# A graph network kernel: one 128-node window per tile of edges, one-hots made by ScalarE, and duplicates and degrees moved from the relational loop into the attention loop

## What is computed

```python
deg = segment_sum(ones, dst); hw = einsum('nd,rdf->rnf', h, weight_r)
M = segment_sum(hw[etype, src] / deg[dst], dst)              # layer 0, relational
updated = relu(0.2 * h + 0.8 * M)
...
e = tanh(concat(h[src], h[dst]) @ W_attn.T + b_attn) @ w_out # layer 1, attention
alpha = softmax of e over the edges of one dst
z = segment_sum(alpha * h[src], dst)
...
deg = segment_sum(edge_weight, src); w = -dis[src] * edge_weight * dis[dst]
# layer 2: two Chebyshev propagations with w, gates, tanh; layer 3: one more propagation
```

## Time and profile before

| | us |
|---|---|
| median of the runs | 2011.47 |
| lowest, highest of 3 | 2008.94, 2014.19 |
| span of the profiled execution | 2533.2 |

### The profile page before, as it was taken

How to read it: one execution, slowest core, us unless ns; L and a number is a source line. 1 busy time by engine, 2 the same in 40 slices (tenths; PEclk the granted TensorE clock), 3 DMA queues, 4 the chain that set the end, 5 groups by cost and what they waited for, 6 DMA issues and landing times.

```text
span 2533.2 us, 28723 instructions
## 1 busy us (share of the span) xinstructions
PE 1374.4 (54%) x7844; PEld 1089.7 (43%) x7845; DVE 991.2 (39%) x2889; ACT 200.8 (8%) x390; POOL 1235.7 (49%) x1381
## 2 busy tenths in 40 slices
PE   4455555565621556566555651111111898879877
PEld 2455554554511456556555640000000898434423
DVE  7555554554604333334333440000000676300488
ACT  2000000000000111111111100000000111000200
POOL 1666666666672366565666677677777000000000
PEclk8766767677755555555555555555555898899989
DMA  5444343435200222222222200000000002988878
GB/s 165 150 155 153 120 152 118 150 121 168 65 1 0 68 63 66 65 62 64 66 66 64 66 21 0 0 0 1 0 0 0 0 0 103 353 335 353 326 295 336
DMA packets 154645, 272.07 MB, mean 107 GB/s; under 512 B 44030, under 2 KB 100154, under 8 KB 151546
## 3 DMA queue, kind: packets, MB, share of 16 engines
q1 hardware_dynamic: 111322, 229.57, 24.9%
q0 software_dynamic: 40064, 41.32, 6.6%
q10 hardware_dynamic: 3232, 0.82, 0.1%
HBM read 215.32 MB, written 56.29 MB: 107 GB/s over the span
## 4 chain that ended last, share of the span: by engine, by line
another core or an unknown queue 28%; PE 26%; issue 20%; DVE 14%; POOL 5%; DMA 4%; DVEq 1%; ACT 1%; SPq 1%; POOLq 0%; ACTq 0%
PE acc L987 10%; PE acc L1035 7%; POOL rings L736 5%; PE acc L1029 4%; DVE rings L1367 2%; DVE big L1826 2%; DMA big<-pairs_by_src 2%; DVE rings L1401 2%; DVE rings L1402 1%; DVE big L1391 1%; DMA rings<-local_rows 1%; PE acc L1009 1%; DMA relation_rows<-big 1%; DMA rings<-relation_rows,idx_ring 1%
## 5 line engine op out<-in xcount | busy, mean ns | idle before, releaser
L987 PE MATMUL acc<-rings 128*65 128x128 f32 x3328 | 576.1, 326 | 634.4 <-issue 459.6
L987 PEld LDWEIGHTS acc<-rings 128*65 128x65 f32 x3328 | 456.0, 168 | 709.4 <-issue 694.3
L736 POOL DMA_INDIRECT rings<-relation_rows,idx_ring x416 | 409.5, 984 | 281.9 <-issue 184.1
L736 POOL DMA_INDIRECT rings<-attention_rows,idx_ring x416 | 394.6, 948 | 305.1 <-issue 234.3
L1029 PE MATMUL acc<-attend_mem,rings 128*128 x1664 | 373.8, 411 | 266.2 <-issue 182.3
L1029 PEld LDWEIGHTS acc<-attend_mem,rings 128*128 128x128 f32 x1664 | 367.3, 328 | 273.0 <-issue 273.0
L753 POOL DMA_INDIRECT pairs_by_src<-fed_val,fed_idx x416 | 405.6, 975 | 149.4 <-issue 120.0
L1425 DVE TENSOR_SCALAR rings<-iota_bf,col_local,score 128x256 f32<-128x256 bf16 x416 | 139.4, 408 | 480.3 <-remote 371.8
L786 POOL DMA_INDIRECT big<-support_rows,ext_node x4 | 3.9, 963 | 450.6 <-DMA support_rows<-big 449.7
L1680 DVE TENSOR_TENSOR rings<-acc,rings 128x512 f32<-128x512 f32 x52 | 35.6, 684 | 352.0 <-remote 343.9
L1035 PE MATMUL acc<-big,attend_mem 128*64 128x512 f32 x700 | 163.0, 600 | 9.1 <-DMA big<-pairs_by_src 9.1
(11 more groups left out here) (279 smaller groups left out, 895.0 us busy)
## 6 DMA issues: line engine op xcount, KB each, us to landing
big<-pairs_by_src SPq DMA_DIRECT2D x54, 2048.0 KB, 12.5
pairs_by_src<-zeros SPq DMA_DIRECT2D x24, 1792.0 KB
big<-key_rows SPq DMA_DIRECT2D x52, 512.0 KB
rings<-local_rows SPq DMA_DIRECT2D x52, 256.0 KB
big<-pairs_by_src SPq DMA_DIRECT2D x12, 1024.0 KB, 12.3
rings<-relation_rows,idx_ring POOLq DMA_INDIRECT x416
pairs_by_src<-fed_val,fed_idx POOLq DMA_INDIRECT x416
rings<-attention_rows,idx_ring POOLq DMA_INDIRECT x416
```

The lines of the kernel that those rows point to most:

```text
L736: pool.indirect_dma_start(ring[h][:, u, 0:width], None, table, bass.IndirectOffsetOnAxis(ap=idx_ring[h][:, u:u + 1], axis=0),).then_inc(ga ...
L987: m = pe.matmul(node_sums[:, bass.ds(at[u] * P + w * P, P)], rows[h][:, u, :], onehot[h][:, u, w * P:(w + 1) * P], start=False, stop=False ...
```

## The change

- A tile's window starts at its own first destination, not at its block, and is 128 nodes wide. The sums lie in eight PSUM banks that overlap by 128 columns (384 new ones each), so that a window never crosses a bank; `turn_nodes` adds the overlaps (57 matmuls for 50). Relational and aggregation loop: one matmul of 128 columns per tile for two.
- In the relational loop ScalarE makes the one-hots, as relu(1 - |window place - column|): eight Abs instructions of 128 elements and one Relu of 1024 in a half-step. DVE has no work in the loop but the duplicates of the first 64 tiles (`early_dups`: three instructions of 1024 elements in each of 8 half-steps).
- Duplicates and degrees of all tiles move to the attention loop: DVE compares keys in one instruction of 1024 elements, makes the one-hot of the source's lower part in another, of its block in one of 200 and multiplies three of 200; PE adds 8 + 8 matmuls to each half-step; SP adds 512 KB of keys; ScalarE adds two small copies. Duplicates are all written to the same cell with the same sum; `indices` and the dump cells are gone.
- The look-up is one matmul of 128 columns per tile for two of 64. It fetches both blocks' numbers, and DVE picks by a predicated copy of 512 elements. One DVE instruction of 1024 elements makes the eight tiles' one-hots, for eight instructions of 256.
- In the aggregation loop DVE makes six of the eight weighted one-hots, ScalarE two (two Abs, two Relu).
- The zeroing writes 896 KB in each half-step for 1792 KB in each loop turn. The degrees' square roots move behind the aggregation loop.

```diff
@@ add_up
-                            block_at[0:1, bass.ds(it * (2 * H) + h * H, H)], ...
+                            sum_at[0:1, bass.ds(it * (2 * H) + h * H, H)], ...
...
-                            for w in range(2):
-                                m = pe.matmul(node_sums[:, bass.ds(at[u] * P + w * P, P)], rows[h][:, u, :],
-                                              onehot[h][:, u, w * P:(w + 1) * P], ...
+                            m = pe.matmul(node_sums[:, bass.ds(at[u], P)], rows[h][:, u, :], onehot[h][:, u, :], ...
-                        if key == "rel":
-                            pe.wait_ge(dups_read, it * 2 + h + 2)
-                            for u in range(H):
-                                m = pe.matmul(dup_bank[:, u * 7:(u + 1) * 7], eq[h][:, u, :], ...
@@ ScalarE, relational loop
+            def window_hots(it, h):
+                act.wait_ge(rows_free["rel"], it * 4 + 2 * h + 2)
+                for u in range(H):
+                    o = act.activation(onehot[h][:, u, :], iota_bf[:, 0:P], ACT.Abs, scale=-1.0,
+                                       bias=col_window[:, bass.ds(it * (2 * H) + (h * H + u), 1)])
+                o.then_inc(away_ready, 1)
+                act.wait_ge(away_ready, it * 2 + h + 1)
+                act.activation(onehot[h], onehot[h], ACT.Relu, scale=-1.0, bias=1.0).then_inc(onehot_ready["rel"], 1)
@@ look_up
                         for u in range(H):
+                            m = pe.matmul(found[h][:, u * 2 * D:(u + 1) * 2 * D], onehot_t[h][:, u * P:(u + 1) * P], there, ...
                         m.then_inc(slot_free[key], 1)
+                        pe.wait_ge(hots_ready, it * 2 + h + 2)
+                        for u in range(H):
+                            pe.matmul(degree_bank, onehot_lo[h][:, u, :], hi_parts[h][:, u, :], ...
+                        for u in range(H):
+                            m = pe.matmul(dup_bank[h][:, u, :], eq[h][:, u, :], parts_ring[h][:, u, :], ...
+                        m.then_inc(degrees_added, 1)
@@ score_step, behind the one-hots of the next half-step
+                    take_dups(it, h)
+                    tile_hots(it, h)
                     dve.wait_ge(gathered["att"][h], (it + 1) * (16 * H))
                     dve.wait_ge(slot_free["att"], it * 2 + h + 3)
+                    dve.copy_predicated(both[:, :, 0], upper_ring[h][:, :].unsqueeze(2).to_broadcast([P, H, D]), both[:, :, 1]
+                                        ).then_inc(picked, 1)
+                    dve.wait_ge(picked, it * 2 + h + 1)
+                    dve.tensor_tensor(msg[h][:, :, :], both[:, :, 0], rows2[h][:, :, 0:D], ALU.add).then_inc(bank_read, 1)
@@ tile_hots
+                dve.wait_ge(keys_here[h], (it + 1) * 16)
+                dve.tensor_tensor(eq[h], key_ring[h], key_cols[:, cols].unsqueeze(2).to_broadcast([P, H, P]),
+                                  ALU.is_equal).then_inc(keys_read, 1)
...
+                dve.tensor_tensor(onehot_lo[h], iota_bank.unsqueeze(1).to_broadcast([P, H, P]),
+                                  col_lo[:, cols].unsqueeze(2).to_broadcast([P, H, P]), ALU.is_equal)
@@ POOL
+            scatter(EARLY, T, dup_val[:, H:], dups_ready, EARLY // H + 5, 2 * IT + 1)
@@ weighted_hots
-                        for u in range(H):
+                        for u in range(BY_DVE):
```

More of the change, by code:

```diff
@@ L56, in gnn_kernel @@
     VB = N // P
+    SPAN = BANK - P
+    TOP = VB * P
+    SUM_BANKS = 8
+    assert SUM_BANKS * SPAN == TOP and SPAN % P == 0 and NODES == TOP + P
+    PER_SPAN = SPAN // P
     SLOTS = 6
@@ L367, in gnn_kernel @@
         sums_taken = {k: sem(f"sums_taken_{k}") for k in sum_passes}
-        dups_read = sem("dups_read")
+        early_read = sem("early_read")
+        early_here = [sem(f"early_here{h}") for h in range(2)]
+        early_eq_ready = sem("early_eq_ready")
+        early_ready = sem("early_ready")
+        away_ready = sem("away_ready")
+        neg_ready = sem("neg_ready")
+        weighted_away = sem("weighted_away")
+        hots_by_act = sem("hots_by_act")
+        key_cols_ready = sem("key_cols_ready")
+        parts_ready = sem("parts_ready")
+        dups_ready = sem("dups_ready")
+        degrees_added = sem("degrees_added")
+        hots_ready = sem("hots_ready")
+        degree_taken = sem("degree_taken")
         rows_copied = sem("rows_copied")
@@ L967, in clear_sums @@
                     pe.wait_ge(wait, 2)
-                for i in range(MAIN + 1):
+                for i in range(SUM_BANKS):
+                    if key == "agg" and i == SUM_BANKS - 1:
+                        pe.wait_ge(expo_ready, 1)
                     m = clear(banks[i])
-                    if i >= MAIN - 1:
+                    if key == "agg" and i >= SUM_BANKS - 2:
                         m.then_inc(slot_free[key], 1)
@@ L1001, in add_up @@
-                        m.then_inc(slot_free[key], 1)
+                            m = pe.matmul(node_sums[:, bass.ds(at[u], P)], rows[h][:, u, :], onehot[h][:, u, :],
+                                          start=False, stop=False, skip_group_check=True)
+                            if key == "rel" and u % (H // 2) == H // 2 - 1:
+                                m.then_inc(rows_free[key], 1)
+                        if key == "agg":
+                            m.then_inc(slot_free[key], 1)
@@ L1015, in look_up @@
                 for h in range(2):
-                    pe.matmul(work[2 + h][:, :], zeros[:, 0:P], zeros[:, :], start=True, stop=True
-                              ).then_inc(slot_free[key], 1)
+                    for i in range(2):
+                        m = pe.matmul(found[h][:, i * BANK:(i + 1) * BANK], zeros[:, 0:P], zeros[:, :], start=True, stop=True)
+                    m.then_inc(slot_free[key], 1)
+                clear(product_bank)
+                clear(banks[3]).then_inc(degrees_added, 2)
                 with pe.Fori(0, IT) as it:
```

451 lines of the change are left out of this document (238 added, 213 removed).

## The result

The changed kernel takes 2024.4 us (median of 7 runs, 2019.5 to 2028.1), the kernel before beside it 2012.6 (7 runs): ratio 1.0063, 95% interval 1.0046 to 1.008. It is slower by 0.6%, where 1976 was forecast.

A forecast was written before the change was run, and what follows sets the result against it. POOL's indirect DMAs were taken as the bound, with the scatter's line ending last. From 2011 us, relational waits -25, shorter gathers -15, early duplicates +2 and late landings +3 made -35: 1976 us, range 1907 to 2042.

The forecast's parts named there:

- The rebuilt time: Whole kernel before, summed from POOL's pace without the profile's stretch: 1952 us, 59 under the median.
- the crawl: PE's matmuls 1.7 us apart in the profile's late scatter, taken as absent unprofiled; rival "partly real": 1907 us, chance 0.12.
- Relational waits, -25 us: Relational loop: POOL's waits for PE shrink with fewer matmuls; 25 us gained, between 0 and 59.
- hidden: Rival, relational loop: POOL already at its pace, so no waits to gain; 2001 to 2011 us, chance 0.20.
- Gathers, -15 us, as DVE leaves: Relational loop: gathers fall from 984 to 948 ns without DVE's work; 15 us gained, between 0 and 15.
- ScalarE's one-hots, zeroing, degrees' arithmetic, the early duplicates: about 0: Relational loop and after: one-hots 3.6 us per half-step under POOL's 10.3, zeroing and degrees 0, early duplicates +2 us.
- Attention loop, 0 to +3 us: Attention loop: DVE 8.4 and PE 7.3 us fit under POOL's 10.0 per half-step; 3 us added for late landings.
- DVE-bound: Rival, attention loop: DVE sets the pace, 11.2 us per half-step; 2038 us, chance 0.15.
- lock: Rival, attention loop: one long DVE instruction stops POOL's DMAs, 52 x 0.7 us; 2012 us, chance 0.08.
- Late scatter: 0.: Late scatter: waits once for the last duplicates, due before its first 16 tiles end; cost 0.
- The aggregation's half-steps: Aggregation loop: 2.9 us for 3.5 to 5.7 per half-step, worth 0 because the scatter's line ends later.
- Landing 3: After POOL's last late scatter: its landing counted as 3 us in the rebuilt time, with the tail unchanged.

The follow-up runs named there:

- e2: Kernel before with duplicates and degrees left out of its relational loop, both window matmuls per tile kept: 2001.0 us against 2013.7, ratio 0.9935.
- the two cures: Changed kernel with the attention loop's three 1024-element DVE instructions cut into four each, and padding edges over 64 rows: 1993.1 us against 2011.6, ratio 0.9915.
- e10c: Changed kernel, padding over 64 rows, attention loop's look-up one-hot in halves of 512, its other two long DVE instructions in quarters: 2003.7 us against 2012.7, one run.

## Why the prediction was wrong

- **The rebuilt time.** The first step was sound in that the profile's 522 us could not be in the runs. But I took the crawl for a thing of profiling. On some chips the runs without a profile take 2525 us too, and that profile and the runs of 2011 us look to be of different chips. The rebuilt line fell 60 us short in pieces all over (relational loop 551 for 534, early scatter 93 for 85, attention 526 for 519, late scatter 485 for 459, landing and tail 301 for 296), and I booked the gap as "waits". Part of it was a wrong rate: the late scatters take 1007 ns on these chips, where the first profile had 975.
- **Relational waits, -25 us.** The step that failed first, the largest term of the sum. It was worth nothing: the 10.1 us put down to PE are 33 of the usual pauses of 0.3 us, and e2 shows that the loop reaches 527.5 with all of the window's matmuls. The reading behind it was wrong as well: of the "98 us of waits for PE" in the first profile 72.2 were "remote", which the rows' own legend calls unexplained. The rival "hidden" had this right (0.20).
- **Gathers, -15 us, as DVE leaves.** Right in that the gathers get shorter when this work leaves, and worth 20: 999 to 950 ns. With 4 us of a shorter gap the loop gained 24.4, of the 40 forecast. That this stands near the 25 of the term above is chance.
- **ScalarE's one-hots, zeroing, degrees' arithmetic, the early duplicates: about 0.** Right: windows +2 in the head, +1.2 in the early scatter, and ScalarE is busy 190.38 / 52 = 3.7 us per half-step for the 3.6 worked out.
- **Attention loop, 0 to +3 us.** The account of engines held: DVE busy 350.65 / 52 = 6.7 us per half-step where I had 8.4, PE 228.71 / 52 = 4.4 where I had 7.3, and DVE waited for landings. "DVE-bound" was wrong on these chips. The 3 us for late landings came out as 3.7 us of longer gaps, by another cause. What failed is the sentence that no lock shows: I had the rival, the instruction and the row for it, and gave it 0.08, because eight short ones showed none. Its price of 0.7 us per half-step was too high: 7.7 to 11.4 us in the loop, 0.15 to 0.2 each.
- **Late scatter: 0.** +2.8, with no wait for duplicates: right. The aggregation's half-steps fell to 113.6 / 52 = 2.2 us and gave nothing, as said:

```profile
1250.70:1364.30 113.60, 102.36 (x831) 91.14 (x832) 84.71 (x310) 101.24 (x257) 88.55 (x108) 0.98 0.02 1
```

- **"Landing 3", before and after.** The step that turned the sign, and no rival had it. The diff says that duplicates all go to one cell; I costed what the duplicates take from DVE and SP, and never asked which tile has many duplicates and when it is scattered. It is the last one, 123 to a cell, and the whole tail waits for it: +12.8 in the windows, 17 in medians. The range's 1907 to 2042 held the time; its middle didn't.

With the two cures the changed kernel is 2011.6 - 1993.1 = 18.5 us under the kernel before. By the windows, whose spans lie 22.9 apart, that is the relational loop's 24, less 2 in the head and 4 in the attention loop and late scatter, and 5 us that aren't the change's: the padding over 64 rows lands 5.6 us sooner than the dump cells did.

## What to carry to other kernels

Where POOL's queue of indirect DMAs is the bound, what counts on DVE is the form of an instruction, not its busy time: merge no tensor_scalar from SBUF to SBUF into one long instruction beside them (in the attention loop 256 elements cost nothing, 1024 some 0.2 us each), while a tensor_tensor with a PSUM operand could be long. Short ones are no safe conduct: in the relational loop of the kernel before 24 of them per half-step went with 20 us of longer gathers. And cutting has a price where POOL waits for DVE, as on the slower chips. Look for padding before letting duplicates write to one cell: it sits in the last tile, and its landing is what everything behind a scatter waits for. And set a profile's span against the runs it is to explain: where they differ, take a second profile before working out a rest from it.

## What the runs showed of the hardware that was not expected

- Writes of one indirect DMA to one address land one after another, 0.13 to 0.16 us each (18.2 to 21.0, 9.7, 2.2 us for 123, 62, 2 in a cell), and those to two cells go on at the same time. The packets are finished in the trace long before the semaphore's last updates. The Trainium skill ("DMA: Bandwidth & Descriptors", Rules for kernel authors) says that each duplicate's write goes out on its own; the landings agree.
- Two sorts of chips: of six medians of the kernel before (2013.7, 2011.6, 2525.1, 2526.5, 2012.7 and the result's 2012.6), taken on different chips at different times, two lie 25% higher, with the result turned round: 0.6% slower here, 2.7% faster there. No chip was used twice, so it is not shown that it is the chip, and not something else at that time, that makes the difference.
- On chips of the first kind POOL stops at the same three places in every loop of gathers, 112 indirect DMAs or seven loop turns apart and counted anew in each loop, waiting for nothing that the profile shows. A stop takes 2.0 to 2.6 us, or 3.7 to 6.1 in loops that hold the duplicates' and degrees' work (the relational one before, the attention one after); the longer ones make up to 8 us in a loop (e10c).
